# An expert loop on one core: TensorE takes the down block ahead of the inner transposes, ScalarE evicts the result ahead of the inner rows

## What is computed

```python
gate = jax.lax.ragged_dot(xs, w_gate, group_sizes)
up = jax.lax.ragged_dot(xs, w_up, group_sizes)
down = jax.lax.ragged_dot(jax.nn.silu(gate) * up, w_down, group_sizes)
...
routed = (down[unsort].reshape(T, K, H) * tkw[..., None]).sum(axis=1)
```

## Time and profile before

| | |
|---|---|
| runs | 1012.5 us median of 3 (1011.89 to 1016.03) |
| profiled execution, its own time | 1009.42 us |
| its span | 1007.7 us |
| mean granted TensorE clock | 0.94 |
| busy share of TensorE, VectorE, ScalarE, GpSimd | 90%, 57%, 50%, 45% |

### The profile page before, as it was taken

The page is one execution under the profiler, slowest core; times in us unless marked ns, Lnnn a source line. Parts: engine busy times, 40 slices in busy tenths (PEclk is TensorE's granted clock), DMA queues, the critical chain, the costliest instruction groups (busy, mean ns, idle before and its releaser), DMA issues.

```text
span 1007.7 us, 21989 instructions
## 1 busy us (share of the span) xinstructions
PE 905.1 (90%) x4596; PEld 489.2 (49%) x4597; DVE 576.2 (57%) x1285; ACT 501.0 (50%) x994; POOL 448.7 (45%) x348
## 2 busy tenths in 40 slices
PE   4358798897969999999999999999999999999994
PEld 1143354544534555555555555555555555555542
DVE  5868798897886443446353455444455555463321
ACT  4376482752224444456454464545556455464331
POOL 1131011110033566555656665646465564566653
PEclk8569878898879999999999999999999999999998
DMA  4122021111228678878878888887788888787864
GB/s 155 42 80 80 1 85 54 43 46 42 93 84 270 155 177 191 184 170 222 185 168 192 180 186 196 169 221 171 175 219 204 234 187 235 174 187 127 147 114 77
DMA packets 90268, 149.25 MB, mean 148 GB/s; under 512 B 9649, under 2 KB 46769, under 8 KB 90225
## 3 DMA queue, kind: packets, MB, share of 16 engines
q0 software_dynamic: 33120, 80.64, 40.3%
q1 hardware_dynamic: 57104, 68.13, 21.2%
HBM read 101.55 MB, written 47.20 MB: 148 GB/s over the span
## 4 chain that ended last, share of the span: by engine, by line
PE 58%; issue 4%; DVE 3%; ACTq 2%; ACT 2%; DVEq 2%; POOL 0%; POOLq 0%
PE bank L258 49%; PE bank L1490 5%; PE bank L1481 3%; ACTq L1158 1%; ACT gu L240 1%; DVEq L1158 1%; DVE hid L1391 1%; DVE gu L247 1%; DVE mark_p L400 0%; DVE mark_q L407 0%; DVE dn L250 0%; ACTq L240 0%; DVEq L247 0%; DVE hid L309 0%; POOL out_dram L1201 0%
## 5 line engine op out<-in xcount | busy, mean ns | idle before, releaser
L258 PE MATMUL bank<-gu,xgT 128*128 x1764 | 404.8, 379 | 1.4 <-issue 1.4
L1201 POOL DMA_INDIRECT out_dram<-y,ids_i x145 | 236.4, 1630 | 233.3 <-DMA out_dram<-y,ids_i 120.5
L1383 DVE TENSOR_TENSOR xgT<-bank,xgT 128x512 f16<-128x512 f32 x148 | 102.2, 691 | 283.2 <-ACT xgT L1244 233.8
L258 PEld LDWEIGHTS bank<-gu,xgT 128*128 128x128 f16 x1764 | 172.4, 98 | 176.9 <-issue 1.6
L258 PE MATMUL bank<-dn,hT 128*128 x870 | 211.7, 379 | 0.8
L1189 POOL DMA_INDIRECT xg<-xrows,ids_i x153 | 167.0, 1092 | 68.3 <-issue 42.4
L1244 ACT CAST xgT<-bank 128x512 f16<-128x512 f32 x148 | 86.9, 588 | 135.6 <-issue 128.5
L1269 ACT ACTIVATE y<-bank 128x512 f32<-128x512 f32 x145 | 87.2, 601 | 110.1 <-PE bank L258 93.0
L258 PEld LDWEIGHTS bank<-dn,hT 128*128 128x128 f16 x870 | 84.9, 98 | 75.3 <-issue 7.8
L1250 ACT ACTIVATE silu<-bank 128x256 f32<-128x256 f32 x147 | 56.1, 382 | 97.7 <-PE bank L258 85.4
L1391 DVE SCALAR_TENSOR_TENSOR hid<-bank,xg,silu 128x256 f32<-128x256 f32 x147 | 70.6, 480 | 59.1 <-ACT silu L1250 52.7
(11 more groups left out here) (217 smaller groups left out, 793.4 us busy)
## 6 DMA issues: line engine op xcount, KB each, us to landing
stage_gu<-in_L_ffn_w_gate_dram SPq DMA_DIRECT2D x32, 512.0 KB
stage_gu<-in_L_ffn_w_up_dram SPq DMA_DIRECT2D x32, 512.0 KB
stage_dn<-in_L_ffn_w_down_dram SPq DMA_DIRECT2D x32, 512.0 KB
x_sb<-in_x_dram SPq DMA_DIRECT2D x4, 1024.0 KB, 6.7
xrows<-adj SPq DMA_DIRECT2D x4, 1024.0 KB, 4.2
out_dram<-acc SPq DMA_DIRECT2D x4, 1024.0 KB, 4.6
xg<-xrows,ids_i POOLq DMA_INDIRECT x153
out_dram<-y,ids_i POOLq DMA_INDIRECT x145
```

Source lines behind the costliest of these rows:

```text
L258: last = nc.tensor.matmul(out_ap, stationary(a, c), moving(w, c), start=(c == 0 and (a, w) == parts[0]), stop=(c == chunks - 1 and (a, w) ...
L1201: g_.indirect_dma_start(out, bass.IndirectOffsetOnAxis(ap=ids_i[:, t:t + 1], axis=0), y[:, t % YS, :], None, compute_op=ALU.add).then_inc( ...
L1383: v.tensor_tensor(xgT[:, s, 1, :, :], bank[XB[s]][:, :].rearrange("p (k t) -> p k t", k=KC), xgT[:, s, 0, :, :], ALU.subtract).then_inc(S[ ...
```

## The change

In a step, TensorE now does `down_of(t - 1)` and then `hidden_T(t)`, where it did them the other way round. ScalarE does `result(t - 1)` and then `hidden(t)`. VectorE, GpSimd and the DMA queues are as they were. The same holds for the two steps ahead of the loop.

```diff
                     gates(t + 1, 1 - s)
-                    hidden(t, s)
                     if not (isinstance(t, int) and t < 1):
                         result(t - 1, 1 - s, (i + 1) % YS)
+                    hidden(t, s)
...
                     e_down = info_of(pe, 0, 0)
-                    hidden_T(t, t)
                     if t:
                         down_of(t - 1, 1 - t, e_down)
+                    hidden_T(t, t)
...
                     e_down, e_next = info_of(pe, 0, t - 1), None if last else info_of(pe, 0, t + 2)
+                    down_of(t - 1, 1 - s, e_down)
                     hidden_T(t, s)
-                    down_of(t - 1, 1 - s, e_down)
                     return e_next
```

## The result

The changed kernel took 1031.9 us in the median of 4 runs (1029.49 to 1032.11), the kernel before, on the same chip, 1013.77 (4 runs): ratio 1.0172, with a 95% interval of 1.0144 to 1.0201. On another chip it was 1029.64 us against 1015.41: 1.0147 [1.0125, 1.0168]. The change is slower, by 1.5 to 1.7%. The forecast of slower was right and so was the place; the time of 1022.7 us and its range, which ended at 1029, were too low.

The account below looks back on a forecast made before the run. TensorE's own order and few pauses were taken to bound the loop. 6.6 + 4.2 - 0.2 - 0.4 = +10.2 us on 1012.5 gave 1022.7 us, range 1016 to 1029.

Parts of the forecast that it names:

- plain steps: Loop steps without splitting of a new expert's weights: the change moves no time, each keeps 4.54 us.
- weight steps: The 30 loop steps where ScalarE and VectorE also split a new expert's weights; TensorE's pauses fall there.
- Term 1: TensorE, weight steps: inner transposes, free before, are paid after the down block, 0.22 us each step, 6.6 us.
- Term 2: ScalarE: y starts 0.22 us earlier, hT's copy follows it 0.49 us later, row copies do not shift.
- Term 3: VectorE: hT 1.25 us later delays xgT and weight subtractions; 0.14 us per weight step, 4.2 us.
- Term 4: Last scatter 0.2 us earlier; transposes fill some pauses at row transposes, 0.4 us saved, bounds 0 and 0.9.
- From the sum to the time: Profiled 1009.4 us plus 10.2 gives 1019.6; the runs' median, 1012.5, is 3.1 above the profiled time: 1022.7.
- the down block did not fill the wait for hid: Rival: on TensorE the down block runs during the wait for hid, up to 13.6 us saved, 998.9 us; 6%.
- TensorE did not pass the waiting block: Rival: transposes start while the down block waits, so their cost vanishes, 1016.1 us; 8%.
- VectorE did not become late in plain steps: Rival: longer register loads make VectorE late in every step, 0.1 us in 115 plain steps, 1034 us; 5%.

Follow-up runs that it names:

- one load less: The change, but VectorE keeps the expert number loaded for the next step, two register loads for three in seven of eight loop steps: 1024.49 us, 1.0076.
- early loads: ScalarE's two next-step loads taken ahead of y in three of four steps, VectorE two loads for three: kernel before 1006.71 us, 0.9905; the change 1018.46, 1.0027.
- the weights last: Splitting of a new expert's weights moved to the end of the step on ScalarE and VectorE: kernel before 1095.28 us, 1.0752; the change 1090.01, 1.0696.

## Why the prediction was right, and where it was wrong

- **What bounds the kernel, and plain steps**: right in the main. TensorE's pauses in weight steps are where the time is made, and all but nine plain steps kept 4.54 us. Six transposes side by side saved nothing. In the weight step of the earlier trace rows the inner transposes were not held back, as the prediction has it: the gate/up block starts at 621.36, and 2.59 later is 623.95. Only the weight load waited there, so the 13.6 us of that list is not TensorE's loss at the transposes, which was 7.8 by starts.
- **Term 1, transposes in the open** (predicted 6.6 us): right in kind, as 634.31 to 634.53 shows, and the price from starts held, not the 273 ns of a record. No run takes this term out alone, but the kernel with one load less comes near to leaving it alone: its subtractions start nearly as early as before, and its pauses in weight steps are 20.2 us, for 14.2 before: 6.0 more, 0.20 per step.
- **Term 2, ScalarE**: right. hT's copy follows y 0.49 us behind it as worked out, and the row copies did not shift, as said: 1.42 us behind the gate/up block's start in the weight steps before, 1.37 after. ScalarE's timeline in the changed kernel:

```profile
624.90 0.60 ACT L1269 ACTIVATE y<-bank 128x512 f32<-128x512 f32 x1 [0.91 <-PE bank L258]
625.39 0.37 ACT L1262 CAST hT<-bank 128x256 f16<-128x256 f32 x1
```

- **Term 3, the later VectorE** (predicted 0.14 us per weight step, 4.2 us): the mechanism was right, the size a little low. The 30 pauses before the down block in weight steps come to 25.6 us in the mean of two executions, where the two blocks had 14.2 before: 11.4, which is 0.38 per step for 0.36 predicted. Less 0.22 for the transposes, 0.16 is the later VectorE: 4.8 us. In a plain step hT starts 1.25 us later against the gate/up block, exactly as forecast (639.94, 0.43 behind the block at 639.51; before 616.00, 0.82 ahead of it at 616.82). Sized too low was the way from hT to xgT: 2.4 us in the mean and 2.30 in the step shown (639.94 to 642.24), not 2.1.
- **A term that was put at nothing: TensorE's own register loads.** "In a plain step the change should move no time at all" is the step of the sum that failed. Nine pauses of 0.04 to 0.37 us stand before the down block in plain steps in each of the two executions, 1.4 and 1.6 us together (0.1 before). VectorE is not late in them: hT had ended 1.7 to 2.7 us earlier. In each, the last register load of TensorE, which stands ahead of the down block, had ended only 0.61 to 0.64 us before it. One such step of the changed kernel (the timeline from 737.5 to 747 us, cut at the end of the down block's fourth matmul; then the loads on TensorE's queue, of which the first took 0.89 us and the second ended at 745.55):

```profile
743.26 2.75 PE L258 MATMUL bank<-gu,xgT 128*128 x12
...
743.70 0.42 DVE L1400 TENSOR_TENSOR hT<-bank,hT 128x256 f16<-128x256 f32 x1 [0.63 <-issue]
...
746.19 1.03 PE L258 MATMUL bank<-dn,hT 128*128 x4 [0.17 <-issue]
```

```profile
L1158 PEldq TENSOR_LOAD <-tile_info x2: 304/598/893, 743.9 to 745.2; - x2
```

  Before, the transposes stood between those loads and the down block and gave it 0.22 us more.
- **Term 4, small returns**: the tail gave its 0.2 us (17.4 to 17.15). The 0.4 at row transposes did not come: pauses there are 1.7 and 1.8 us in the loop before, 1.7 and 1.8 after.
- **From the sum to the time**: the other step that failed. The terms as measured (6.6 + 4.8 + 1.3, less 0.2) make 12.5 us for 10.2, and 1012.5 + 12.5 = 1025.0 us lies inside the range. But 1012.5, the median of three runs, was low: in the five comparisons the kernel before had medians of 1013.8 to 1018.6 us, and single runs from 1008.4 to 1021.0; all 63 of these runs have a median of 1015.4, 2.9 above it, and the nine runs of the change 1030.0. The range had no room for this scatter. From 1015.4 the terms as measured would make 1027.9; the last 2 us to 1030.0, and 4 to the 1031.9 of the first comparison, were not traced to a place. Between two executions of one kernel the start of the loop alone differs by 4 us.
- **Rivals**: the down block did not fill the wait for hid, as hid still ends before hT; TensorE did not pass the waiting block; VectorE did not become late in plain steps.

What stays open: why the new order still costs 15 us of the loop with early loads (651.2 for 636.3). By starts, 8.2 us of it are pauses in weight steps, which hold the transposes and a still later hT, 2.6 are pauses at down blocks in plain steps, and 2.5 stand at row transposes. No run splits the 8.2.

## What to carry to other kernels

Work that runs inside a stall is free only while it stands ahead of the instruction that waits; moved behind it, it is paid in full, and that price is read from the starts of the records, all taken from one view. A queue's register loads are a piece of the order like any instruction: look for the place where the engine waits anyway, and ask of each pause whether another engine or the engine's own loads ended it. To credit a cost to them, take them out of both orders. The ratios of two parts add up only if the stage that they change says so. And a sum of differences should be added to a time with the scatter of the kernel before, taken from as many runs as there are.

## What the runs showed of the hardware

**Ahead of the loop the granted clock differs between executions, and the start of the loop with it.** From 200 to 310 us the profiles of the kernel before read 0.87 and, in the second, 0.82 (columns as in the earlier trace rows):

```profile
200.00:310.00 110.00, 93.10 (x518) 50.69 (x517) 94.00 (x274) 35.13 (x63) 21.57 (x15) 0.87 0.23 76
```

```profile
200.00:310.00 110.00, 94.55 (x501) 52.33 (x502) 93.33 (x273) 36.22 (x65) 18.84 (x13) 0.82 0.20 68
```

Its loop began at 309.7 and 313.8 us; the change's at 313.6 with 0.82 and at 309.5 with 0.87. That is 4 us of scatter that no edit made, of the size of the terms argued about here. Of all 18 profiles nine read 0.81 to 0.83, with the loop from 312.0 to 314.5 us, and nine 0.86 or 0.87, from 309.5 to 312.3. Which of the two brings the other is not shown.

**A long pause can cost twice.** In the kernel with the weights last TensorE ran before the pause at granted clock 1.00, which is its level of 2.4 GHz, and idled 2.4 us. In the 4.3 us behind it the clock was 0.60, so most of that block ran at the 1.2 GHz level, and then it was 1.00 again:

```profile
616.00:620.40 4.40, 4.40 (x25) 2.42 (x24) 2.30 (x3) 4.25 (x7) 2.53 (x2) 1.00 0.68 117
...
623.50:627.80 4.30, 4.27 (x12) 1.74 (x13) 1.25 (x3) 0.00 (x0) 2.31 (x2) 0.60 0.88 254
629.70:632.30 2.60, 2.60 (x15) 1.28 (x13) 0.64 (x1) 1.01 (x2) 1.37 (x1) 1.00 0.48 143
```

The block took 4.45 us for 2.75: 1.70 more, on top of the pause. Not every such pause had this price: of 26 pauses of 2.1 to 2.7 us before the gate/up block in this kernel, 16 were followed by a block that was 1.2 us or more longer from start to start, and of 26 of 1.7 to 2.7 us in the change with the weights last, 9. The pauses of the change itself, 1.7 us at most, left the down block at its 1.29 us from start to start.

**A register load** takes 0.31 us in the median, and three with their checks follow each other at 0.65 us (from hT to xgT, 625.9 to 627.2 in this row of VectorE's queue in the change):

```profile
L1158 DVEq TENSOR_LOAD <-tile_info x3: 301/304/309, 625.9 to 627.2; - x3
```

The Trainium skill, page "DMA: Bandwidth & Descriptors", section Latency and other measured facts, gives a floor of about 600 ns for such a load. The trace differs as to the load itself, at half of that, and comes near it only for a load together with its checks.
